# Deeper one-hot and PSUM buffering for two gather loops of a graph-and-experts kernel

## The reference, cut to what matters

```python
# x: 6250 x 256; src, dst: 200000 edges of a first graph, sorted by dst
xn  = layernorm(x)
x   = x + relu(xn @ W + segment_sum((xn @ M)[src], dst))      # first graph
xn2 = layernorm(x)
# second graph: 131072 unsorted edges
h     = xn2 @ W_gat                                            # 16 features a node
e     = leaky_relu(a_src[src] + a_dst[dst])                    # 4 heads
ee    = exp(e - segment_max(e, dst))
agg   = segment_sum(h[src] * ee / segment_sum(ee, dst), dst)
gates = softmax of the best 2 of 4 scores made of agg
out   = x + sum over 4 experts of gate * (gelu(xn2 @ W1 + b1) @ W2 + b2)
```

## Time and profile before

| what | value |
|---|---|
| runs | 3730.53 us median, 3729.65 to 3742.68 |
| profiled execution | 3737.18 us, of which the trace spans 3736.0 us |
| granted PE clock, mean | 0.868 of full speed |
| busy: PE, DVE, POOL, ACT | 73%, 58%, 63%, 24% of the span |
| visits, until DVE's last running sum | about 82 to 2565 us |
| blocks, PE's first to DVE's last | about 2672 to 3574 us |

### The profile page before, as it was taken

How to read it: one execution, slowest core, us unless ns; L and a number is a source line. 1 busy time by engine, 2 the same in 40 slices (tenths; PEclk the granted TensorE clock), 3 DMA queues, 4 the chain that set the end, 5 groups by cost and what they waited for, 6 DMA issues and landing times. The chain is left out here.

```text
span 3736.0 us, 43909 instructions
## 1 busy us (share of the span) xinstructions
PE 2727.2 (73%) x13434; PEld 1990.3 (53%) x13459; DVE 2184.5 (58%) x5820; ACT 905.5 (24%) x1563; POOL 2367.7 (63%) x2799
## 2 busy tenths in 40 slices
PE   2556777777767777678777787787877877787935
PEld 1334555555545545455555555555646656565924
DVE  5677676676665554555554555553124666565857
ACT  3000111111122222211111111111223444444623
POOL 4666666666666666556666666668886788787040
PEclk9676988889888888889998989898978999998968
DMA  9676565666656666666666666665131111111146
GB/s 290 209 255 197 183 203 181 200 192 187 204 183 199 197 194 193 188 187 199 196 209 205 191 202 203 201 199 154 30 99 35 50 38 51 40 44 51 41 141 218
DMA packets 476808, 601.25 MB, mean 161 GB/s; under 512 B 72486, under 2 KB 415390, under 8 KB 474526
## 3 DMA queue, kind: packets, MB, share of 16 engines
q1 hardware_dynamic: 378766, 375.94, 31.0%
q0 software_dynamic: 97216, 219.88, 21.2%
q10 hardware_dynamic: 592, 2.64, 0.2%
HBM read 313.06 MB, written 286.79 MB: 161 GB/s over the span
## 5 line engine op out<-in xcount | busy, mean ns | idle before, releaser
L1710 POOL DMA_INDIRECT ring<-xn_d,srci x1611 | 1560.4, 969 | 932.2 <-DVE ring L822 439.3
L1509 PE MATMUL wide<-ring,one_hot 128*128 128x256 f32 x3222 | 986.4, 442 | 487.1 <-DVE ring L822 349.7
L822 DVE SCALAR_TENSOR_TENSOR ring<-ring,same_v,wide 128x256 f32<-128x256 f32 x1610 | 770.4, 479 | 953.2 <-remote 438.8
L1509 PEld LDWEIGHTS wide<-ring,one_hot 128*128 128x128 f32 x3222 | 666.6, 219 | 767.5 <-issue 306.9
L1618 PE MATMUL wide<-tab_parts,low_hot 128*128 128x208 bf16 x6288 | 719.4, 266 | 181.4 <-issue 132.9
L1618 PEld LDWEIGHTS wide<-tab_parts,low_hot 128*128 128x128 bf16 x6288 | 575.7, 102 | 325.2 <-issue 261.8
L1759 POOL DMA_INDIRECT g<-tab_d,srt x500 | 494.2, 988 | 82.2 <-issue 80.4
L1557 PE MATMUL wide<-xt,w1s 128*128 128x512 f32 (+1 forms) x832 | 423.9, 638 | 1.5 <-DVE feat L787 0.8
L1567 PE MATMUL wide<-w2s,hh 128*128 128x256 f32 x1568 | 411.8, 410 | 7.6 <-issue 3.9
L1242 ACT ACTIVATE hh<-wide,b1c 128x512 f32<-128x512 f32 (+1 forms) x208 | 137.8, 662 | 1121.9 <-PE wide L1557 513.2
L1567 PEld LDWEIGHTS wide<-w2s,hh 128*128 128x128 f32 x1568 | 327.8, 210 | 73.5 <-issue 15.2
(11 more groups left out here) (370 smaller groups left out, 1862.5 us busy)
## 6 DMA issues: line engine op xcount, KB each, us to landing
run_d<-ring SPq DMA_DIRECT2D x201, 1024.0 KB
ring<-xn_d,srci POOLq DMA_INDIRECT x1611
y_d<-yo SPq DMA_DIRECT2D x196, 128.0 KB
comb<-y_d SPq DMA_DIRECT2D x28, 896.0 KB
low_row<-low_d SPq DMA_DIRECT2D x13, 1024.0 KB
sum_d<-g SPq DMA_DIRECT2D x15, 768.0 KB
g<-tab_d,srt POOLq DMA_INDIRECT x500
xn_d<-ring SPq DMA_DIRECT2D x7, 896.0 KB, 7.1
```

The lines of the kernel that those rows point to most:

```text
L822: dve_at["run", j] = step(V.scalar_tensor_tensor(out=o, in0=ring[:, (j - 1) // JC % RING, (j - 1) % JC, :], scalar=same_v[:, j:j + 1], in1 ...
L1509: T.matmul(wide[:, 4 + j // 2 % 2, j % 2 * D:(j % 2 + 1) * D], one_hot[:, j // 4 % 4, j % 4, :], ring[:, j // JC % RING, j % JC, :], start ...
L1710: G.indirect_dma_start(out=ring[:, s, j % JC, :], out_offset=None, in_=xn_d, in_offset=at_rows(srci[:, j:j + 1])).then_inc(sem(f"gather{s} ...
```

## The change

The change has two parts.

In the blocks there are now four sets of one-hot matrices (`DEPTH = 4`) and four pairs of PSUM banks (`BLOCK_BANK`: 4 and 5, 6 and 7, 0 and 1, 2 and 3). DVE and ACT build a set two blocks ahead instead of one (`AHEAD = 2`). PE needs block `b - 4` out of its banks where it needed `b - 2`.

In the visits a pair has one signal, given by its second matmul, where each visit had one; DVE waits once a pair. From pair 493 on (visit 986, 13 visits after the last step of the row search) the pairs go round four banks, 4, 5, 2 and 3, so PE waits for the pair four before it. The first uses of banks 2 and 3 wait for the last step of the search.

```diff
+WIDE_LAG = 13
+DEPTH = 4
+AHEAD = 2
+BLOCK_BANK = (4, 6, 0, 2)
...
-    low_hot = q.take("low_hot", [P, 2, 4, LOW], BF16)
+    low_hot = q.take("low_hot", [P, DEPTH, 4, LOW], BF16)
...
+    wide_from = (sort_end + WIDE_LAG) // 2
+    pair_bank = [4 + p % 2 if p < wide_from else (4, 5, 2, 3)[(p - wide_from) % 4] for p in range(PAIRS)]
+    pair_ahead = [max([q for q in range(p) if pair_bank[q] == pair_bank[p]], default=-1) for p in range(PAIRS)]
...
-                V.wait_ge(sem("visited"), min(j // 2 * 2 + 2, V_))
-                o, more = ring[:, c % RING, j % JC, :], wide[:, 4 + j // 2 % 2, j % 2 * D:(j % 2 + 1) * D]
+                if j % 2 == 0:
+                    V.wait_ge(sem("visited"), j // 2 + 1)
+                o, more = ring[:, c % RING, j % JC, :], bank[pair_bank[j // 2]][:, j % 2 * D:(j % 2 + 1) * D]
...
-            if b >= 2:
-                V.wait_ge(sem("picked"), b - 1)
+            if b >= DEPTH:
+                V.wait_ge(sem("picked"), b - DEPTH + 1)
...
-                if b + 1 < NBLOCKS:
-                    low_columns(b + 1)
+                if b + AHEAD < NBLOCKS:
+                    low_columns(b + AHEAD)
...
-            if done % 4 == 2 and done // 4 + 1 < NBLOCKS:
-                low_quarter(done // 4 + 1)
+            if done % 4 == 2 and done // 4 + AHEAD < NBLOCKS:
+                low_quarter(done // 4 + AHEAD)
...
-            if j >= 4 and j % 2 == 0:
-                T.wait_ge(dve_step, dve_at["run", j - 3])
-            T.matmul(wide[:, 4 + j // 2 % 2, j % 2 * D:(j % 2 + 1) * D], one_hot[:, j // 4 % 4, j % 4, :],
-                     ring[:, j // JC % RING, j % JC, :], start=True, stop=True).then_inc(sem("visited"), 1)
+            p = j // 2
+            if j % 2 == 0 and pair_ahead[p] >= 0:
+                T.wait_ge(dve_step, dve_at["run", 2 * pair_ahead[p] + 1])
+            elif j % 2 == 0 and p >= wide_from:
+                T.wait_ge(dve_step, dve_at["low_rows"])
+            mm = T.matmul(bank[pair_bank[p]][:, j % 2 * D:(j % 2 + 1) * D], one_hot[:, j // 4 % 4, j % 4, :],
+                          ring[:, j // JC % RING, j % JC, :], start=True, stop=True)
+            if j % 2 or j == V_ - 1:
+                mm.then_inc(sem("visited"), 1)
...
-                            if b >= 2:
-                                T.wait_ge(dve_step, dve_at["taken", b - 2])
+                            if b >= DEPTH:
+                                T.wait_ge(dve_step, dve_at["taken", b - DEPTH])
```

More of the change, by code:

```diff
@@ L343, in build @@
     SHIFTED, SMALL, SCORES = 0, 64, 256
+    PAIRS = -(-V_ // 2)
     def last_of(c):
@@ L856, in split_table @@
             yield
-            low_columns(0)
+            for b in range(AHEAD):
+                low_columns(b)
             yield
@@ L863, in low_columns @@
             V.wait_ge(sem(f"low_in{c % 2}"), sent(c // 2))
-            if b >= 2:
-                V.wait_ge(sem("picked"), b - 1)
+            if b >= DEPTH:
+                V.wait_ge(sem("picked"), b - DEPTH + 1)
             at = block_in[b] * LOW
             for q_ in range(4 - ACT_QUARTERS):
-                dve_at["low_hot", b] = step(V.tensor_scalar(low_hot[:, b % 2, q_, :], low_row[:, c % 2, at:at + LOW],
+                dve_at["low_hot", b] = step(V.tensor_scalar(low_hot[:, b % DEPTH, q_, :], low_row[:, c % 2, at:at + LOW],
                                                             lane[:, q_:q_ + 1], None, ALU.is_equal))
@@ L877, in pick @@
                 V.wait_ge(dve_step, dve_at["pick", b - 1])
-            half = 2 * (b % 2)
+            first = BLOCK_BANK[b % DEPTH]
             dve_at["taken", b] = then(V.tensor_tensor(
                 picked[:, :, :, :],
-                wide[:, 4 + half:6 + half, :].rearrange("p c (k x) -> p (c k) x", k=2)[:, :, 0:HX * HI].rearrange(
+                wide[:, first:first + 2, :].rearrange("p c (k x) -> p (c k) x", k=2)[:, :, 0:HX * HI].rearrange(
                     "p k (f h) -> p k f h", h=HI),
@@ L1313, in low_quarter @@
                              bias=lane_n[:, 3 - i:4 - i]).then_inc(sem("far_off"), 1)
-            if b >= 2:
-                A.wait_ge(sem("picked"), b - 1)
+            if b >= DEPTH:
+                A.wait_ge(sem("picked"), b - DEPTH + 1)
             for i in range(ACT_QUARTERS):
                 A.wait_ge(sem("far_off"), ACT_QUARTERS * b + i + 1)
-                A.activation(low_hot[:, b % 2, 3 - i, :], far_off[:, b % 2, i, :], ACT.Relu, bias=ones[:, 0:1],
+                A.activation(low_hot[:, b % DEPTH, 3 - i, :], far_off[:, b % 2, i, :], ACT.Relu, bias=ones[:, 0:1],
                              scale=-1.0).then_inc(sem("low_quarter"), 1)
@@ L1326, in scalar_program @@
             if done == 0:
-                low_quarter(0)
+                for b in range(AHEAD):
+                    low_quarter(b)
             done += 1
-            if done % 4 == 2 and done // 4 + 1 < NBLOCKS:
-                low_quarter(done // 4 + 1)
+            if done % 4 == 2 and done // 4 + AHEAD < NBLOCKS:
+                low_quarter(done // 4 + AHEAD)
             if done in weighed_at:
@@ L1617, in matrix_gathers @@
                             for q_ in range(4):
-                                mm = T.matmul(bank[4 + 2 * (b % 2) + i // 2][:, at:at + HX * HI],
-                                              low_hot[:, b % 2, q_, i * P:(i + 1) * P],
+                                mm = T.matmul(bank[BLOCK_BANK[b % DEPTH] + i // 2][:, at:at + HX * HI],
+                                              low_hot[:, b % DEPTH, q_, i * P:(i + 1) * P],
                                               tab_parts[:, k, q_, :, :].rearrange("p f h -> p (f h)"),
```

## The result

| kernel | median us | ratio to before, 95% interval |
|---|---|---|
| before | 3736.74 | |
| changed | 3706.05 | 0.9929 (0.9908 to 0.995) |

The change makes the kernel 0.7% faster. By the medians that is 31 us and by the ratio 27 us, where 66 us were forecast. The direction was right and the size was more than twice too large. The profiled execution of the changed kernel has a span of 3703.5 us.

The account below looks back on a forecast made before the run. The prediction took a loop of waits (gather, matmul, running sum, gather), not an engine's speed, as the bound. Visits 50 us plus blocks 16 us made 66 us, 3730.53 − 66, say 3665 us; range 3575 to 3748.

Parts of the forecast that it names:

- Between the ends I go by who was late when DVE waited.: Visits from 986: DVE's waits without "remote", 160.8 of 385 us, set the share of PE's 147.7 us bank waits gained.
- The lower bound: Visits from 986: four banks gain 0 us, because DVE's late signal comes at the same moment anyway.
- the chunk of the earlier trace: Visits near 2013 us: PE stands 3.04 us for a bank; DVE gets the signal 3.6 us after the row's end.
- the prediction's own signs: Forecast wrong if visits after 1612 us end under 15 us earlier or the stretch before moves over 10 us.
- The share left out of its range: Chance that the time falls outside 3575 to 3748 us, put at some 0.17.
- It had been met already: Visits: DVE's second sum of each pair loses a wait that was already met, counted as no gain.
- The signals on PE's side: Visits: 805 fewer PE signals, taken as 0 us because PE's rows show no price for one.
- The blocks: Building matrices two blocks ahead removes PE's waits for one-hot matrices: 16 of 26.1 us gained, last stretch's 5.9 us nothing.
- Nothing comes of it: Rival: every bank wait returns one step on, POOL's 175.5 us of waits for sums stay; 3725 us, chance 0.15.
- Fewer signals make the late ones fewer: Rival, all visits: half the signals take a third of the lateness, 146 us, 3519 us; a tenth 44 us; chance 0.11.
- Slower: Rival, visits: denser POOL gathers make the 224.2 us of remote waits grow; at +50% 3777 us; chance 0.13.
- The clock: Rival, later visits: going round four banks drops the granted clock from 0.90 to 0.83; 3728 us, chance 0.05.

Follow-up runs that it names:

- quiet_two_banks: quiet_visits with two PSUM banks instead of four in the visits; a visit takes 1.09 us against 1.07 with four.
- one_wait: The kernel before, but DVE waits once a pair, at its first sum, and every visit keeps its signal; 0.9954 to before.
- one_signal: The kernel before, but PE gives one signal a pair and DVE still waits at both sums; 0.9993 to before.
- quiet_visits: The changed kernel, but from visit 1024 on POOL does a short memset instead of each gather; a visit takes 1.07 us for 1.51.
- LEAD 24: The changed kernel with POOL allowed 24 places ahead of the running sum instead of 14; 1.0275 to the kernel before.
- pause_pairs: The changed kernel with a 0.33 us memset on POOL ahead of every second gather of the visits; 0.9925 to the kernel before.
- pause_lead18: The changed kernel with pause_pairs' memsets and POOL allowed 18 places ahead of the running sum instead of 14; 0.9831 to the kernel before.

## Why the prediction was wrong in size

**The step that failed: "Between the ends I go by who was late when DVE waited."** This gave 0.42 × 147.7 = 62 us, then 50; measured are 8 us by the ratio and 9 to 11 by the stages. Two things were wrong in it. It took PE's bank wait as a cause, to be shared out by DVE's waits; but PE waited for DVE, and DVE for PE's late signal, so most of it was the same lateness seen from the other side, as `quiet_two_banks` shows. And it took DVE's 160.8 us without "remote" as starts of PE that a bank would bring forward. They became 181.2 us. By the rows' ends, DVE stood 139 us before the pair's row had ended and stands 137 us now: PE starts late for gathers and units instead. The lower bound, the chunk of the earlier trace rows, was the nearer one.

That chunk itself was read a little wrong. PE's row of four at 2012.13 is one pair, two matmuls to a visit, and the pair that DVE adds at 2016.88 is the one before it, of this row, which ended at 2011.93:

```profile
2010.90 1.03 PE L1509 MATMUL wide<-ring,one_hot 128*128 128x256 f32 x4
```

So that signal was 4.9 us late; the 3.6 us are counted from the next pair's end. By the prediction's own signs it failed as well: the visits after 1612 us got 12 us shorter in the profile, less than 15, and the stretch before them moved by 15 us, more than 10. (The share left out of its range is 0.12 by its own chances, not 0.17; this changes nothing here.)

**"It had been met already": a second, smaller miss to the other side.** The second wait of a pair was put at nothing. It costs 68 ns in each of 805 pairs (DVE's second sum starts 104 ns after the first has ended with the wait, and 36 ns without, medians over the trace), 55 us of DVE's time. `one_wait`, which takes just this away, is 17 us faster (0.0046 of 3754). The sum lies in front of what POOL waits for; that this is why a part of the 55 us arrives is argued and not shown.

**The signals on PE's side: zero, as forecast.** The Trainium skill, "TensorE: Matmul & The Clock Gate", section "The cost: per-tile semaphore tail", has a cost of 26.3 ns for each increment behind a group of tiles packed into the array; an estimate from it for 805 increments is 21 us. `one_signal` takes away just these and is 0.9993, by its interval 9 us faster at most; here the measurement decides. That PE's idle time, 206 us from visit 986 on, covers what an increment costs is argued: no run measures one increment by itself.

**The blocks: about the size that was forecast.** 16 us forecast; 18 by the ratio (its interval goes from 9 to 27), 13 by the stages. PE's waits in the blocks of the changed kernel, whole stage:

```profile
PE wide L1635 <- issue: 149.6, 461, 1.2
PE wide L1635 <- DVE low_hot L879: 0.5, 2, 0.3
```

The 26.1 and 5.9 us of the earlier trace rows are gone. DVE's remote waits for picks stayed: 323.4 us in the whole stage before, 323.8 now.

**The rivals.** "Nothing comes of it" was nearly right for the banks, and its sign was written down: POOL's waits for sums stayed at 165.8 us. DVE's remote row did not grow by what PE's lost, but that row was no measure; by the rows' ends its late time grew from 267 to 285 us. What this rival left out is that the blocks and the saved wait still made the kernel faster. "Fewer signals make the late ones fewer" falls with `one_signal`: a tenth of them gone was to give 44 us, where the interval allows 9, and by the rows' ends DVE's late time before visit 986 is 302 us there for 277 in the kernel before. "Slower" did not come about, for POOL did not get denser: it is busy for 591 of 941 us, 595 of 953 before. But more late signals with longer runs of gathers are what LEAD 24 shows. The clock did not fall: 0.91 for 0.90. By the rule of the Trainium skill, "TensorE: Matmul & The Clock Gate", section "A second HAM failure mode: psum-queue depth-cycling", it might have; this trace does not bear that out.

## What to carry to other kernels

Before a buffer is made deeper, follow the wait for it one step further. If the engine that frees it stands for a late signal of the one that waits, the buffer's wait is that lateness over again, and depth moves it to the next wait in line. The cheapest test is to take the suspected source of the lateness away, and then the buffers, as `quiet_visits` and `quiet_two_banks` do. And a wait that is always met was not free here on an engine inside the loop: measure its price and count it.

## What was not expected of the hardware

- PE's signals come late while POOL issues indirect gathers, and mostly come out when it stops: 33 of 38 long waits ended 1.4 us or more after POOL's last gather, and none was left without gathers. Whether POOL's issuing or the transfers themselves hold them up was not separated. The bytes moved don't seem to decide: in the blocks all transfers together move 46 GB/s, in the visits 199, and DVE's remote waits are 174.9 us in 543 and 224.2 in 953.
- A second wait ahead of one instruction, which had been met already, cost DVE 68 ns.
- POOL could take 266 us more work in the visits without any change in time (`pause_pairs`).
- On one chip the kernel before took 3596 us instead of some 3730 to 3750. In `pause_lead18` there, the blocks took 772 us from first to last pick, in the profiles on other chips 868 to 904; the visits before 986 were only 2% shorter. DVE's remote waits for picks there were 199.5 us for 323.8, and the granted clock 1.00 for 0.89; which of these is cause and which effect stays open.
